# Turning the keys' and queries' stacked parts with fp32r products, a tile of their own for the squares, and a shared buffer for the gates

## The reference, cut to what matters

```python
q = _l2norm((x @ Wq + bq).reshape(B, S, NH, HD))   # 16 heads of 8
k = _l2norm((x @ Wk + bk).reshape(B, S, NH, HD))
state = q
for _ in range(STEPS):                             # two steps
    att = jax.nn.softmax(jnp.einsum('bqhd,bkhd->bqhk', state, k), axis=-1)
    state = jnp.einsum('bqhk,bkhd->bqhd', att, v)
...
h = jax.nn.silu(xe @ w1[e]) * (xe @ w3[e])         # xe: tokens times their gate for expert e
```

## Time and profile before

| | before |
|---|---|
| median of 3 runs | 3548.38 us (3545.81 to 3549.18) |
| the profiled execution | 3555.46 us, span of its instructions 3553.7 us |
| granted TensorE clock, mean | 0.961 of 2.4 GHz |
| PE busy | 3247.1 us, 91% |
| DVE busy | 2401.4 us, 68% |
| ACT busy | 2082.6 us, 59% |
| POOL busy | 1219.1 us, 34% |

### The profile page before, as it was taken

How to read it: one execution, slowest core, us unless ns; L and a number is a source line. 1 busy time by engine, 2 the same in 40 slices (tenths; PEclk the granted TensorE clock), 3 DMA queues, 4 the chain that set the end, 5 groups by cost and what they waited for, 6 DMA issues and landing times.

```text
span 3553.7 us, 55360 instructions
## 1 busy us (share of the span) xinstructions
PE 3247.1 (91%) x19974; PEld 1682.0 (47%) x19974; DVE 2401.4 (68%) x5281; ACT 2082.6 (59%) x2689; POOL 1219.1 (34%) x2291
## 2 busy tenths in 40 slices
PE   5888998989999899999999999999999999998999
PEld 2444444444444444454444445444444444444567
DVE  2636675847678676767767676776867677775662
ACT  2454666656666666666666666566666656564442
POOL 3314242342424334242522424252342425222321
PEclk8989999989999999999999999999999999998999
DMA  1000000001110100111001011110001111000110
GB/s 41 4 28 5 31 4 29 31 4 34 31 34 28 31 9 30 34 32 34 29 31 34 5 34 31 34 31 28 34 4 34 31 34 32 30 29 4 59 33 34
DMA packets 81502, 96.89 MB, mean 27 GB/s; under 512 B 50544, under 2 KB 68400, under 8 KB 81104
## 3 DMA queue, kind: packets, MB, share of 16 engines
q1 hardware_dynamic: 81232, 93.35, 8.2%
HBM read 82.76 MB, written 4.78 MB: 25 GB/s over the span
## 4 chain that ended last, share of the span: by engine, by line
PE 53%; DVE 15%; ACT 14%; POOL 10%; issue 7%; SPq 1%; DMA 0%; ACTq 0%; DVEq 0%; POOLq 0%
PE ps L679 14%; PE ps L696 13%; ACT probs L810 12%; PE ps L751 7%; DVE negmax L1041 6%; PE ps L761 5%; PE ps L579 5%; PE ps L716 3%; PE ps L585 2%; PE ps L574 2%; DVE uts L1007 1%; POOL qT L1235 1%; POOL xe L1258 1%; POOL qk L1199 1%; DVE stats L907 1%
## 5 line engine op out<-in xcount | busy, mean ns | idle before, releaser
L810 ACT ACTIVATE probs<-ps 128x1024 f32<-128x1024 f32 x1536 | 1574.6, 1025 | 1070.6 <-PE ps L679 1056.2
L1041 DVE TENSOR_REDUCE negmax<-ps 128x2 f32<-128x1024 f32 x1024 | 1249.6, 1220 | 468.4 <-PE ps L716 451.9
L679 PE MATMUL ps<-qT,kT 32*128 32x512 f32 x3072 | 786.5, 507 | 109.8 <-ACT probs L810 57.4
L696 PE MATMUL ps<-probs,v 128*32 128x512 f32 x6144 | 851.8, 627 | 0.0
L1258 POOL TENSOR_TENSOR xe<-xT_m,G 128x512 f32<-128x512 f32 x288 | 367.2, 1278 | 1045.3 <-PE ps L751 997.2
L751 PE MATMUL ps<-xe,w_sb 128*128 128x256 f32 x2304 | 668.2, 416 | 7.9 <-DVE hid L1100 4.1
L679 PEld LDWEIGHTS ps<-qT,kT 32*128 32x128 f32 x3072 | 291.9, 185 | 763.8 <-ACT probs L810 493.7
L716 PE MATMUL ps<-kT,qT 32*128 32x512 f32 x2048 | 529.4, 512 | 93.7 <-DVE negmax L1041 90.1
L751 PEld LDWEIGHTS ps<-xe,w_sb 128*128 128x128 f32 x2304 | 406.8, 196 | 185.3 <-issue 136.9
L1098 DVE SCALAR_TENSOR_TENSOR th<-th,ps 128x256 f32<-128x256 f32 x576 | 236.8, 411 | 216.6 <-ACT th L840 214.2
L840 ACT ACTIVATE th<-ps 128x256 f32<-128x256 f32 x576 | 221.7, 385 | 180.4 <-PE ps L751 170.1
(11 more groups left out here) (169 smaller groups left out, 2652.8 us busy)
## 6 DMA issues: line engine op xcount, KB each, us to landing
G<-gates_dram SPq DMA_DIRECT2D x96, 768.0 KB, 6.2
maxrow<-negmaxT SPq DMA_DIRECT2D x512, 2.0 KB
v<-v_tok SPq DMA_DIRECT2D x256, 18.0 KB, 1.9
X<-in_x SPq DMA_DIRECT2D x16, 256.0 KB, 2.9
out<-X SPq DMA_DIRECT2D x16, 256.0 KB, 2.3
w_sb<-in_w SPq DMA_DIRECT2D x1, 1152.0 KB, 7.0
w_sb<-in_w SPq DMA_DIRECT2D x1, 576.0 KB, 8.7
gates_dram<-gT SPq DMA_DIRECT2D x32, 18.0 KB
```

The costliest lines, as they stand in the source:

```text
L679: nc.tensor.matmul(ps[:, B_ST + h, :], kT[a][rows, g * S + kc * P:g * S + (kc + 1) * P], qT[a][rows, g * S:(g + 1) * S], start=True, stop= ...
L696: ins = nc.tensor.matmul(ps[ROWS * j:ROWS * (j + 1), B_UT, :], v[:, at:at + ROWS], probs[:, n % QUADS, j, :], start=(kc == 0), stop=(kc == ...
L810: nc.scalar.activation(probs[:, quad % QUADS, j:j + 2, :], ps[:, B_ST:B_ST + 2, :], ACT.Exp).then_inc(sem["exp_done"], 1)
L1041: nc.vector.tensor_reduce(negative[:, tc, 2 * half:2 * half + 2], ps[:, B_SM:B_SM + 2, :], AX_X, ALU.max, negate=True).then_inc(sem["sm_re ...
```

## The change

1. The groups of `p0_op` and `p1_op` are made by `matmul` with a unit matrix in fp32r (`turn_operands`) in place of `transpose` with an fp32 one. The stacks are therefore declared fp32r, and the unit matrix `id_r` is written by DVE at the start.
2. `stack0k` can no longer hold fp32 squares: they get a tile `sq` that is half as large, so POOL squares and DVE sums one half (keys), then the other (queries). The second squaring waits for the first sum.
3. To make room, `gT` is gone: the turned gates lie in the buffer of `xe` that the next run of the experts fills first. ACT waits for the last products that read that buffer, and the planner puts `m_gt` behind them.
4. In the planner `p0_op` and `p1_op` cost 0.13 of a slot and not 0.25, and the chain of the first attention starts two slots earlier (`P0_AT`), the feed-forward layer ahead of it one (`FFN0_AT`). Positions of `st`, `sm` and `pv` stay the same. The number of warming groups (products whose result nobody reads, in the first turns) goes from 220 to 229.

```diff
-FFN0_AT, P0_AT, P0_OP_AT = -37, -29.0, (-11, -7, -5, 2.5)
+FFN0_AT, P0_AT, P0_OP_AT = -38, -31, (-11, -7, -5, 2.5)
-COST = {**{n: 0.25 for n in "ffn_xt p0_xt p1_xt o_t m_xt p0_op p1_op turn m_gt m_logits".split()},
+COST = {**{n: 0.25 for n in "ffn_xt p0_xt p1_xt o_t m_xt turn m_gt m_logits".split()}, "p0_op": 0.13, "p1_op": 0.13,
...
-                    ahead = ("m_xe",) + runs[n - 1] + (EX - 1,)
+                    ahead = ("m_gu",) + runs[n - 1] + (NE - 1, 1)
...
-                    pos = max(pos, placed[ahead] + 0.1)
+                    pos = max(pos, placed[ahead] + 0.6)
...
-        t.at(p + 9.4, "p0_squares", b, behind=(("p0_qkv", b, TC - 1), 1.4))
-        t.at(p + 11.5, "p0_sums", b, behind=(("p0_squares", b), 1.8))
+        ahead = ("p0_qkv", b, TC - 1), 1.4
         for i in range(2):
-            t.at(p + 17 + i, "p0_hi", b, i, behind=(("p0_sums", b), 5 + i))
+            t.at(p + 8.4 + 2 * i, "p0_squares", b, i, behind=ahead)
+            t.at(p + 9.4 + 2 * i, "p0_sums", b, i, behind=(("p0_squares", b, i), 1))
+            ahead = ("p0_sums", b, i), 1
+        for i in range(2):
+            t.at(p + 16 + i, "p0_hi", b, i, behind=(("p0_sums", b, 1), 5 + i))
...
+            def turn_operands(key, blocks):
+
+                bank = take_side(key)
+                for i, t in enumerate(blocks):
+                    ins = nc.tensor.matmul(bank[:, i * P:(i + 1) * P], t, id_r[:], start=True, stop=True)
                 ins.then_inc(full_signal(key), 1)
...
-                    act.wait_ge(sem["gates_out"], 16 * n)
-                nc.scalar.activation(gT[:], side_bank(key)[0:EX, :], ACT.Copy).then_inc(read_signal(key), 1)
+                    act.wait_ge(*filled(gu_of[2 * EX * n - 3]))
+                nc.scalar.activation(gates_of(n), side_bank(key)[0:EX, :], ACT.Copy).then_inc(read_signal(key), 1)
...
+            def p0_sums(n, b, i):
+                dve.wait_ge(sem["p0_squared"], n + 1)
+                sums = norm[:, 0, :].rearrange("p (x w) -> p x w", w=2)[:, :, i:i + 1]
+                ins = nc.vector.tensor_reduce(sums, sq[:], AX_X, ALU.add)
+                if i == 0:
+                    ins.then_inc(sem["p0_halved"], 1)
+                    return
+                link(ins)
```

More of the change, by code:

```diff
@@ L360, in build @@
         OT = xT_b
-        stack0 = [sb(f"stack0{n}", [P, TC * NH, ROWS]) for n in "kq"]
-        stack1 = [sb(f"stack1{n}", [P, NH * TC, ROWS]) for n in "kq"]
+        stack0 = [sb(f"stack0{n}", [P, TC * NH, ROWS], F32R) for n in "kq"]
+        stack1 = [sb(f"stack1{n}", [P, NH * TC, ROWS], F32R) for n in "kq"]
         qstack = sb("qstack", [P, TC * NG, ROWS])
@@ L498, in build, with gates_of @@
                 last[PROJECTED[name]] = (name,) + args
+        def gates_of(run):
+            return xe[EX * run % 2][0:EX, :]
         gu_of = {no[key]: key for key in use if key[0] == "m_gu"}
@@ L573, in warm @@
                 for c in range(2):
-                    nc.tensor.matmul(bank[:, c * P:(c + 1) * P], id_sb[:], id_sb[:], start=True, stop=True)
+                    nc.tensor.matmul(bank[:, c * P:(c + 1) * P], id_sb, id_sb, start=True, stop=True)
             def turn_chunks(key, blocks):
@@ L660, in p0_op @@
                 pe.wait_ge(sem["p0_lo"], 2 * b + i + 1)
-                turn_chunks(("p0_op", b, g, i),
+                turn_operands(("p0_op", b, g, i),
                             [stack0[i][:, tc * NH + NG * g:tc * NH + NG * (g + 1), :] for tc in range(TC)])
@@ L665, in p1_op @@
                 pe.wait_ge(sem["p1_lo"], 2 * b + i + 1)
-                turn_chunks(("p1_op", b, c, i), [stack1[i][:, TC * h:TC * (h + 1), :] for h in range(NG * c, NG * c + NG)])
+                turn_operands(("p1_op", b, c, i), [stack1[i][:, TC * h:TC * (h + 1), :] for h in range(NG * c, NG * c + NG)])
             def st(n, kind, b, g, i):
@@ L740, in m_gt @@
                 for tc in range(TC):
-                    ins = nc.tensor.transpose(bank[0:EX, tc * P:(tc + 1) * P], gate[:, tc, :], id_sb[:])
+                    ins = nc.tensor.transpose(bank[0:EX, tc * P:(tc + 1) * P], gate[:, tc, :], id_sb)
                 ins.then_inc(full_signal(("m_gt", b, k)), 1)
@@ L1184, in heads1, with p0_squares, p0_sums @@
                 return stack1[i][:].rearrange("p (h c) e -> p c h e", c=TC)
-            def p0_squares(n, b):
-                pool.wait_ge(*read(("p0_qkv", b, TC - 1)))
-                for i in range(2):
-                    ins = nc.gpsimd.tensor_tensor(heads0(0)[:, :, :, HD * i:HD * (i + 1)], qk_heads(0, i), qk_heads(0, i),
-                                                  ALU.mult)
-                ins.then_inc(sem["p0_squared"], 1)
-            def p0_sums(n, b):
+            def p0_squares(n, b, i):
+                if i == 0:
+                    pool.wait_ge(*read(("p0_qkv", b, TC - 1)))
+                    if b:
+                        pool.wait_ge(sem["p0_summed"], b)
+                else:
+                    pool.wait_ge(sem["p0_halved"], b + 1)
+                nc.gpsimd.tensor_tensor(sq[:].rearrange("p (c h) d -> p c h d", c=TC), qk_heads(0, i), qk_heads(0, i),
+                                        ALU.mult).then_inc(sem["p0_squared"], 1)
+            def p0_sums(n, b, i):
+                if i == 0:
+                    return
                 pool.wait_ge(sem["p0_summed"], b + 1)
```

34 lines of the change are left out of this document (16 added, 18 removed).

## The result

The changed kernel takes 3752.75 us (median of 5 runs, 3712.66 to 3764.68), the kernel before 3548.38 us on the same chip (5 runs, 3545.81 to 3553.06): **1.0555 times the time before, 95% interval 1.0523 to 1.0587**. The forecast was 3570 us, the range 3530 to 3602. It is slower, as forecast, but by 204 us and not by 22. The profiled execution took 3712.66 us and is the quickest of the five, so its rows show some 40 us less than the median; its mean granted clock is 0.919, that of the other four 0.904 to 0.908.

The account below looks back on a forecast made before the run. TensorE, busy for 91% of the span, was taken as the bound. The profiled execution's 3555.5 + 0 (products) + 22 (packing) + 0 (waits) = 3577.5 us, lying 7.1 above the runs' median, gave 3570; range 3530 to 3602.

Parts of the forecast that it names:

- A product in place of a transpose: 0 us: TensorE's groups: an fp32r product block costs about 0.12 us like a transposed one, so 1024 exchanged blocks cost 0 us.
- The rival "the clock": Half-clock stretches beside turned stacks go if products keep the clock up and transposes do not: 3556 us, chance 0.05.
- The slots are packed anew: +22 us: TensorE's slots overfilled or left below the floor by the halved group price: +1.6 us a turn, +22 us in all.
- The places that I named: Two slots of 3.24 us where m_down meets p0_qkv, and 2.96 us for the slot with pv and three groups.
- The waits of the chain: 0: TensorE's waits for POOL's low parts and ACT's side banks: 3.4 us a turn become 3.4 at other places, 0 net.
- The wait for a side bank: Slots 88 to 90: three groups in a row need all side banks, ACT frees them late, a wait of 1.4 us.
- squares in halves cost nothing: POOL and DVE in the first attention's chain: the second half waits for DVE while POOL is idle, costing nothing by itself.
- The rest: Moved m_gt, ACT's new wait and SP's later gate DMAs cost 0; unit matrix and split sums lengthen the start some 0.4 us.
- Products stream at 0.28 a group: Rival for TensorE's groups: the weights' load hides wholly, -14 us over the slots, 3534 us, chance 0.22.
- products cost more: Rival for TensorE's groups: 0.66 us a group gives 3607 us, two passes at 0.93 give 3665; chance 0.12.
- The chain's waits go: Rival: POOL finishes earlier and ACT's copies keep up, so 2 us a turn return on 13 turns: 3544 us, chance 0.15.

Follow-up runs that it names:

- the old plan: The planner's numbers of before (0.25 of a slot for a group, old starts) put back in the changed kernel; with its products 3671.82 us.
- the transposes' kernel in the new plan: The changed kernel with its groups made by transposes with the fp32 unit matrix again, planner's changes kept: 3645.11 us.
- the transposes' kernel in the old plan: The changed kernel with transposes and the planner's numbers of before, leaving squares in halves and shared gates: 3587.18 us.

## Why the prediction was wrong

**A product in place of a transpose: 0 us.** This is the step that failed. The price of a block was right: 0.12 in a stream, as worked out, and the loads of 0.19 (I had taken 0.181, from a load of 32 rows) stay hidden. What I left out is that the exchange can change the speed of everything around it. It cost 85 us in the old plan and 108 in the new one, through the clock: two kernels of one order stand at 0.954 and 0.921, and products over 256 columns at nearly the same distance bring back 71 of 85 and 95 of 108. In the old plan the products' time is all in slots 85 to 95: 34.9 us a turn against 28.4, with 210 against 31 us of half clock in ten turns.

**The rival "the clock"** named the mechanism and had its sign wrong: I priced the case that transposes let the clock fall and products keep it up. It is the other way round. The Trainium skill, page "TensorE: Matmul & The Clock Gate", section "Part 4: PE-mode transpose", says that the full clock does not engage for transposes. The runs disagree: the ten full turns of the kernel before have no half clock at all in slots 85 to 95, where most of the stacks' transposes stand, and with 128-column fp32r products in their place the clock fell further. I had weighed the rule against rows of transposes alone, and no row could speak for the products. I should have bounded the clock from both sides like the price: that rival as it stood ended at 14 us, and its mirror image was in no case.

**The slots are packed anew: +22 us.** The sign was right, the size was not: 58 us. Each sequence's slots, averaged over ten full turns and compared with the kernel before, show where. The places that I named came as worked out: two slots of 3.27 and 3.29 us (3.24 forecast), and 2.92 for the slot with `pv` and three groups (2.96). Slots 88 to 90 last 8.17 (2278.05 to 2286.22), where I said 7.9. But the transposes' kernel in the new plan is 7.1 us a turn above before (4.2 above the transposes' kernel in the old plan, which has the halves too), and not 1.6: slots 58 to 68 give 1.9 (0.3 forecast), slots 69 to 84 give 2.7 (1.0), slots 19 to 34 give 1.1, where I had a gain. The rest are waits that a sum of costs does not hold, and half clock. TensorE's idle time that DVE ends grows from 1.7 to 2.6 us a turn in slots 19 to 34, from 0.2 to 1.0 in slots 58 to 68 and from 0.0 to 1.5 in slots 69 to 84. Slots 58 to 84 have 3.2 us of half clock a turn, where before had none. The changed kernel's time line shows such waits in slots 64, 65, 83 and 84:

```profile
2221.83 1.13 PE L767 MATMUL ps<-xe,w_sb 128*128 128x256 f32 x4 [0.42 <-DVE X L945]
2222.89 0.50 PE L695 MATMUL ps<-qT,kT 32*128 32x512 f32 x2
2224.00 0.50 PE L732 MATMUL ps<-kT,qT 32*128 32x512 f32 x2 [0.60 <-DVE negmax L1061]
...
2262.88 2.20 PE L660 MATMUL ps<-wqkv,xT_b 128*128 128x384 f32 x6
...
2267.43 0.63 PE L588 MATMUL ps<-id_r,uts 128*128 128x128 f32 x4 [0.93 <-DVE v_tok L967]
2267.99 0.50 PE L695 MATMUL ps<-qT,kT 32*128 32x512 f32 x2
2268.81 0.88 PE L660 MATMUL ps<-wqkv,xT_b 128*128 128x384 f32 x2 [0.32 <-DVE v_tok L967]
...
2270.33 1.94 PE L712 MATMUL ps<-probs,v 128*32 128x512 f32 x8
2272.20 1.12 PE L588 MATMUL ps<-id_r,O 128*128 128x128 f32 x4
```

The releaser is DVE each time, an engine whose queue I had looked at for the sums only. In slot 82 TensorE makes three parts of `p1_qkv` in a row (2262.88), and what comes next waits for DVE (0.93 and 0.32). The clock falls behind these waits: `pv` takes 1.87 (2270.33 to 2272.20). The new plan lowers the clock from 0.954 to 0.947 by itself.

**The waits of the chain: 0.** By place wrong, and by sum. The keys' group of `stack0` does not wait for POOL in any of ten full turns of the changed kernel, where I had 1.8 us:

```profile
2252.35 0.50 PE L695 MATMUL ps<-qT,kT 32*128 32x512 f32 x2
...
2272.97 0.76 PE L595 MATMUL ps<-id_r,stack0k 128*128 128x128 f32 x4
2273.65 0.50 PE L695 MATMUL ps<-qT,kT 32*128 32x512 f32 x2
```

```profile
2270.32 0.80 POOL L1232 CAST stack0k<-stack0k 128x512 fp32r<-128x512 f32 x1
```

Slot 77 begins at 2252.35. TensorE comes to the group 20.6 us later, where I had 18.3 (2385.6 less 2367.3); of the 2.3 us, 1.25 are the two waits for DVE above. POOL's last low part is ready at 18.8, where I had 20.0. The wait for a side bank is there (1.79; I had 1.4). That squares in halves cost nothing is refuted: in the old plan they add 37 us, with a wait of 1.66 for the keys' low parts that the kernel before does not have (its slot 86 grows by 2.0 us a turn, of 2.9 in all), and half clock behind it. The early start takes this wait away, and brings DVE waits in its place: with halves, transposes and the early start alone TensorE idles 1.2 us a turn for `v_tok` in slots 69 to 84.

**The rest** was right: the shared gates, 0.9996 [0.9980, 1.0011].

**The other rivals.** *Products stream at 0.28 a group* and *products cost more* are both refuted by the starts in the time line. *The chain's waits go* is half true: those for the low parts went, and others replaced them. That the kernel came out slower, as forecast, is no merit of the sum: the 22 us it rests on are a tenth of what was measured.

**The sum as it came:** 3550 + 37 (halves) + 58 (plan) + 108 (products, through the clock) = 3753, the median of the changed kernel. The parts are differences of medians taken in this order, so they add up by construction, and in another order they differ (products: 85 in the old plan).

What stays open: why 128-column products keep the clock down so much longer than transposes of as many blocks, as far apart. The runs show that it hangs on the form of the instruction, but not on what about it. Nor are the 37 us of the halves divided exactly between the new wait and the clock behind it: of 2.9 us a turn 2.0 lie in slot 86, where the wait is, and 331 against 281 us of half clock bound the clock's share by 25 us.

## What to carry to other kernels

An exchange of one TensorE instruction for another has two prices, its own time and what it does to the clock of its neighbours. The second can be the larger one, so compare the granted clock of a first trial before counting instructions. When a planner's price is lowered, list the waits of each engine that feeds the moved pieces, since sums of costs hold only the bound engine. And a wait can cost more than its length where TensorE falls to half clock behind it.

## What the runs showed of the hardware

- Same order, nearly the same distance of blocks (four in 0.49 to 0.52 us at full clock; transposes and narrow products eight in 1.90 us at half clock): transposes 0.954, fp32r products of 128 columns 0.921, of 256 columns 0.953. The clock separated three instruction forms that the time line at full speed could not.
- An fp32r product of 256 columns with its own weights costs hardly more than one of 128: a group with three wide products and a narrow one takes 0.52 us, a narrow group 0.50.
- A product in fp32 costs two passes (its row counts eight instructions for four blocks), 0.99 us a group, and keeps the clock at 0.947 like transposes in that plan.
- The clock need not fall after a wait, and what follows the wait decides with it: behind about 1.65 us of idle at the same place of the turn there was half clock in ten of ten turns with narrow products, in five with transposes and in two with wide products.
